# First summing stage of a graph network: half of each step's slots summed as f32 products with a widened 0/1 matrix

## The reference, cut to what matters

```python
B = jnp.exp(-edge_attr)
msgs = B[:, None] * x[col]
out = jax.ops.segment_sum(msgs, row, num_segments=N_NODES)
```

## Time and profile before

| what | value |
|---|---|
| median of 3 runs | 5168.92 us |
| lowest and highest run | 5147.55, 5176.96 us |
| span of the profiled execution, first to last instruction | 3717.5 us |
| median run less that span | 1451.4 us |
| TensorE, VectorE, ScalarE, GpSimd busy over the span | 58%, 70%, 21%, 53% |
| first and last low part of the stage (L1237) | 723.4 us, 1017.0 us |

### The profile page before, as it was taken

One profiled execution on the slowest core, in us unless ns is written; L12 is line 12 of the kernel. 1 busy time (PEld: TensorE's weight loads), 2 busy tenths in 40 slices (PEclk: granted clock), 3 DMA queues, 4 the chain that ended last, 5 costly groups with the idle time before them and its releaser, 6 DMA issues. The chain is left out here.

```text
span 3717.5 us, 94213 instructions
## 1 busy us (share of the span) xinstructions
PE 2149.9 (58%) x24555; PEld 1628.6 (44%) x24556; DVE 2606.7 (70%) x5968; ACT 796.1 (21%) x2086; POOL 1984.6 (53%) x1987
## 2 busy tenths in 40 slices
PE   1435777566535555555655553465666666666597
PEld 0225666455534444444544442344444444444232
DVE  3898999888856777776777765477777777777511
ACT  0023555455520111111111110011111111111100
POOL 0112444333327777777777730777777777776000
PEclk9867889756655666666666665566666766666699
DMA  4046777788776667666666630565555555555687
GB/s 148 12 126 170 258 260 261 233 244 237 217 74 184 184 180 190 183 175 183 186 184 182 183 94 9 130 161 146 150 151 144 153 154 148 153 148 147 223 309 282
DMA packets 679457, 646.11 MB, mean 174 GB/s; under 512 B 129015, under 2 KB 513308, under 8 KB 678333
## 3 DMA queue, kind: packets, MB, share of 16 engines
q1 hardware_dynamic: 375773, 346.64, 31.7%
q0 software_dynamic: 77184, 154.07, 17.5%
q10 hardware_dynamic: 226300, 143.41, 12.6%
HBM read 433.64 MB, written 222.40 MB: 176 GB/s over the span
## 5 line engine op out<-in xcount | busy, mean ns | idle before, releaser
L1646 POOL DMA_INDIRECT rows<-nodes_xl,id_slot x832 | 831.1, 999 | 419.3 <-issue 249.5
L1646 POOL DMA_INDIRECT rows<-nodes_kv,id_slot x832 | 825.1, 992 | 290.8 <-issue 244.8
L1842 DVE SCALAR_TENSOR_TENSOR running_counts<-running_counts,same_block,counts_p 128x128 f32<-128x128 f32 x1144 | 393.9, 344 | 412.6 <-PE counts_p L2001 305.7
L2001 PE MATMUL counts_p<-hot_src,hot_blocks 128*128 128x128 bf16 x2288 | 291.9, 281 | 585.8 <-DVE running_counts L1842 584.4
L2001 PEld LDWEIGHTS counts_p<-hot_src,hot_blocks 128*128 128x128 bf16 x2288 | 217.6, 154 | 661.4 <-DVE running_counts L1842 599.4
L2045 PE MATMUL sums<-parts,hot 128*128 128x68 bf16 (+1 forms) x4992 | 325.2, 251 | 250.1 <-DVE parts L1826 250.1
L2045 PEld LDWEIGHTS sums<-parts,hot 128*128 128x128 bf16 x4992 | 311.6, 168 | 271.5 <-issue 271.5
L1091 POOL DMA_INDIRECT msg_by_src<-message,unit_slot x156 | 199.7, 1280 | 311.3 <-DVE message L944 292.4
L1260 PE MATMUL sums<-parts,hot 128*128 128x65 bf16 x3168 | 183.7, 235 | 120.7 <-DVE parts L1237 120.7
L1687 ACT CAST parts<-mixed 128x544 bf16<-128x544 f32 (+1 forms) x208 | 133.0, 639 | 536.1 <-DVE mixed L1810 278.1
L1971 PE MATMUL picked<-rows,ident 128*128 128x512 f32 x208 | 198.2, 1054 | 79.2 <-DMA rows<-nodes_xl,id_slot 68.3
(11 more groups left out here) (490 smaller groups left out, 4289.9 us busy)
## 6 DMA issues: line engine op xcount, KB each, us to landing
hot_src<-hot_src_by_cell SPq DMA_DIRECT2D x1144, 64.0 KB
adjacency<-running_counts ACTq DMA_DIRECT2D x1144, 64.0 KB
hotT<-hotT_by_step SPq DMA_DIRECT2D x208, 256.0 KB
hot<-hot_by_step SPq DMA_DIRECT2D x208, 256.0 KB
blocks<-adjacency SPq DMA_DIRECT2D x40, 1280.0 KB
hot_src_by_cell<-hot POOLq DMA_DIRECT2D x132, 256.0 KB
loc_all<-loc_by_cell SPq DMA_DIRECT2D x104, 256.0 KB
hotT_by_step<-hotT ACTq DMA_DIRECT2D x104, 256.0 KB
```

Of the source, the lines that this page charges most:

```text
L1646: pool.indirect_dma_start(out=rows[:, j, t, :], out_offset=None, in_=table, in_offset=bass.IndirectOffsetOnAxis(ap=ids[:, j, t:t + 1], axis=0)
L1842: v.scalar_tensor_tensor(runs[:, r, q, :], before_it, same[:, bass.ds(J * BBODY + (count_from + q), 1)], counts_p[:, q - HALVES[q >= len(H ...
L2001: ins = nc.tensor.matmul(counts_p[:, q - HALVES[half][0], :], hot_b[:, r, :, t], hot_s[:, r, q, :, g], start=g == 0, stop=g == 1)
```

## The change

Of the 8 slots of a step, slots 0 to 3 (THREE = 4) go on as three bf16 parts. Slots 4 to 7 are multiplied as they arrived, in f32. For that ScalarE writes the `hot` of those four slots out in f32 (`hot_wide`, 128 x 512), in its step J for step J-1, ahead of the middle part. High part, `left`, middle part and low part have half their former size. TensorE makes 4 x 3 bf16 products and then 4 f32 products in a step. As TensorE now reads the arrived rows themselves, `load` waits for `summed` where it waited for `left_made`.

```diff
-                left = sbuf("left", [P, RS, TB, cols], ctx=c)
-                parts = sbuf("parts3", [P, RS, 3, TB, cols], BF16, ctx=c)
+                THREE = 4
+                left = sbuf("left", [P, RS, THREE, cols], ctx=c)
+                parts = sbuf("parts3", [P, RS, 3, THREE, cols], BF16, ctx=c)
+                wide = sbuf("hot_wide", [P, RS, TB - THREE, P], ctx=c)
...
                     if not known(J, RS):
-                        eng.wait_ge(left_made, J - (RS - 1))
+                        eng.wait_ge(summed, J - (RS - 1))
                         eng.wait_ge(ends_taken, J - (RS - 1))
                         eng.wait_ge(located, J - (RS - 1))
...
-                            nc.scalar.copy(parts[:, s, 0, :, :], rows[:, s, :, 0:cols]).then_inc(high_made, 1)
+                            nc.scalar.copy(parts[:, s, 0, :, :], rows[:, s, 0:THREE, 0:cols]).then_inc(high_made, 1)
                         if not known(J, 1):
+                            r = (s - 1) % RS
+                            act.wait_ge(hot_made, J)
+                            nc.scalar.copy(wide[:, r, :, :].rearrange("p (c g) e -> p c g e", g=2),
+                                           hot[:, r, THREE // 2:, :, :].rearrange("p c e g -> p c g e")).then_inc(wide_made, 1)
                             act.wait_ge(left_made, J)
                             nc.scalar.copy(parts[:, (s - 1) % RS, 1, :, :], left[:, (s - 1) % RS, :, :]).then_inc(middle_made, 1)
...
-                            v.tensor_tensor(left[:, r, :, :], rows[:, r, :, 0:cols], parts[:, r, 0, :, :], ALU.subtract).then_inc(left_made, 1)
+                            v.tensor_tensor(left[:, r, :, :], rows[:, r, 0:THREE, 0:cols], parts[:, r, 0, :, :], ALU.subtract).then_inc(left_made, 1)
...
-                        pe.wait_ge(hot_made, J + 1)
+                        pe.wait_ge(wide_made, J + 1)
                         pe.wait_ge(low_made, J + 1)
                         for b, n in enumerate(ns):
                             for t in (2 * b, 2 * b + 1):
+                                if t >= THREE:
+                                    ins = nc.tensor.matmul(sums[:, bass.ds(n, cols)], wide[:, s, t - THREE, :], rows[:, s, t, 0:cols],
+                                                           start=False, stop=False)
+                                    continue
                                 for m in range(3):
```

More of the change, by code:

```diff
@@ L1113, in aggregate @@
                 arrived = [sem(f"arrived{s}", c) for s in range(RS)]
-                located, hot_made, ends_taken, high_made, left_made, middle_made, low_made, summed = (
-                    sem(n, c) for n in ("located", "hot_made", "ends_taken", "high_made", "left_made", "middle_made", "low_made", "summed"))
+                located, hot_made, ends_taken, high_made, left_made, middle_made, low_made, wide_made, summed = (
+                    sem(n, c) for n in ("located", "hot_made", "ends_taken", "high_made", "left_made", "middle_made", "low_made",
+                                        "wide_made", "summed"))
                 own, opened, closed = sem("own", c), sem("opened", c), sem("closed", c)
```

## The result

The changed kernel takes 5438.8 us (median of 4 runs, 5429.8 to 5442.5) against 5166.3 for the kernel before: a ratio of 1.053, 95% interval 1.050 to 1.056. It is slower by 272 us, where 161 were forecast. The direction and the place were right, the size was not, and the time lies outside the range (5245 to 5400).

A forecast was written before the change was run, and what follows sets the result against it. The prediction took ScalarE's list to bound the kernel, VectorE close behind. The moved wait closes a ring, 63 x (7.04 - 4.48) = 161 us, added to 5169 for 5330 us; range 5245 to 5400.

The forecast's parts named there:

- What bounds now: Summing stage: ScalarE's list, two steps long, bounds with no slack (150.4 + 127.7 of 280 us), VectorE close behind.
- The faster rival: ScalarE's 2.20 us gap is elastic, so VectorE or transfers bound: pair 3.67 us, forecast time 5116 us; chance 0.05.
- What gets cheaper, and the widening: `left` and low part fall to 422 ns, high and middle part to 409; ScalarE's added widening takes 616 ns.
- The wait: ScalarE's loads wait for `summed` of J-1, closing a ring: pair 4.48 to 7.04 us, 63 pairs, 161 us more.
- The f32 product: TensorE's f32 products are 0.22 us apart at 1.2 GHz; a slot costs 0.22 where three bf16 products cost 0.165.
- The rule that was set aside: TensorE reloads FP32 weights in every pass: 0.43 us a product, pair about 8.8 us, time near 5430.
- the prediction's own pair: Two steps from `ends` of J at 1.2 GHz: J-1 products start 2.15, J's end 5.54, pair 7.20 us.
- The clock: TensorE's granted clock stays 0.58, about 0.16 of the time at 2.4 GHz, making the pair 7.04 us.
- The 1451 us and SyncE: The 1451 us outside the profiled span stay; SyncE's five issues per pair, now waiting for `summed`, cost nothing.

## Why the prediction was right in direction and wrong in size

**What bounds now: not refuted, and not tested.** ScalarE's list had no slack. No run shows that the stage shortens when it gets some: the two runs on the kernel before that relieve ScalarE hand its issues to SyncE, and in both SyncE's own queue, at 0.78 to 0.79 us an issue, then takes as long as the pair. With its five issues it still waited 43.1 us over the stage. The faster rival took the share of 0.82 for room down to 3.67 us a pair. Over 200 us or more of this stage no run read has more than 0.82 (40 us at its start have 0.86), and the shortest stage is still that of the kernel before. That the transfers can't go beyond this share isn't shown by it.

**What gets cheaper, and the widening: right.** 426 and 423 ns for `left` and low part (422 said), 404 for the high part (409), 614 for the widening (616).

**The wait: right.** It was called the larger term, and alone it costs 218 us. The order of starts in a pair held: first products 2.16 us after `ends` (2.15 said), 0.16 from products to issues (0.1), 1.52 to `ends` (1.56).

**The f32 product: the step that failed.** The prediction read y_new as "six in 1.55 us", "so 0.22 apart", and took 0.22 for a product. 0.22 was right for a record. But its fifty records belong to one product for each tile of 128 nodes, and 3125 nodes are 25 tiles; so a product is two records. In the changed kernel they are 1056 over the stage, for 132 x 4 products. So a product costs 0.44 us at 1.2 GHz, a slot in f32 0.44 where three bf16 products cost 0.165, and a step's issue is 0.66 + 8 x 0.22 = 2.42 us in place of 1.54. Put into the prediction's own pair: step J-1 issues from 2.15 to 4.57, J starts at 4.6, its products end 0.66 + 7 x 0.22 + 0.42 = 2.62 later, at 7.2, and with 0.1 + 1.56 the pair is 8.9. 63 x (8.9 - 4.48) = 278 us, 5447, against 5439 measured. Of the 117 us by which that exceeds the forecast 161, the price makes 63 x (8.9 - 7.2) = 107, and 10 come from taking the pair at 1.2 GHz throughout (7.20 for 7.04).

The rule that was set aside had it. The fast weight load is not used for FP32, by the Trainium skill, "TensorE: Matmul & The Clock Gate", section "Weight-path perf modes"; with the 107 ns for a load from that page's section "LDWEIGHTS" and the four passes of the Trainium skill's page "FP8 and Floating Point Precision", section "TensorE Precision Notes", the estimate was 0.43 us a product, 8.8 us a pair and a time near 5430. The trace has 0.44, 8.86 and 5439. The row did not speak against the rule; it was counted wrongly.

That it isn't the 65 columns which set the pace of a record, the trace of the kernel before shows. Eight f32 products of a later stage have weights of the same form and 128 columns in place of 64, at the same granted clock of 1.00 as the earlier trace rows:

```profile
1520.39 2.05 PE L1987 MATMUL turn_p<-ef_slot,wide_we 128*128 128x128 f32 x16
...
1520.40:1522.20 1.80, 1.80 (x17) 1.80 (x17) 0.62 (x2) 0.00 (x0) 1.38 (x2) 1.00 0.49 121
```

Sixteen records in 2.05 us, of 0.275 at the median, are (2.05 - 0.275) / 15 = 0.118 us apart; the eight records of y_new with 64 columns are (1.10 - 0.275) / 7 = 0.118 apart. Twice the columns cost nothing more. The weights are the same in both, which fits the rule; a fixed cost of a record that has nothing to do with the loads isn't excluded.

**The clock: slightly off.** 0.58 was kept, 0.50 was granted. With 0.16 of the pairs some 2 us shorter, the lower clock cost 20 us at most (an estimate), and on the side of slower than forecast.

**The 1451 us and SyncE: as costed.** The rest of the program is unchanged. SyncE's queue waited 319.5 us for products, but over the whole stage of the changed kernel ScalarE shows no wait for landings and VectorE one, of 0.8 us.

## What to carry to other kernels

When a wait is moved from one producer to a later one, follow it to the head of the issuing engine's list: if that producer depends on work which the same engine did just before, the wait closes a ring, and the buffers do not help unless the load looks ahead by fewer steps. Count records against the products in the code before a duration is taken as the price of one. An f32 product of 65 columns was no bargain against three bf16 ones: it took work from VectorE and gave it to TensorE, for which the loads now waited. And before issues are moved to another queue, see how much that queue still waits: when a run with the move has none of its waits left, the run measures that queue and not the engine that was relieved.

## What the runs showed that was not expected

- One f32 product appears as two weight loads and two matmul records, 0.22 us apart each at 1.2 GHz with 128 x 65 elements moving; three bf16 products of the same shape take 0.165 us. At 2.4 GHz f32 records are 0.118 us apart with 64 columns and with 128.
- The kernel before has executions whose spans differ by 1459 us (3717.5 and 5176.5) while this stage takes 293.6 and 295.9.
- SyncE, which has no other work, issues one of these transfers in 0.78 to 0.79 us, its register loads counted in, where its queue shows no wait for any engine. With seven of eight issues a pair on SyncE the run took 56 us more (5281.0 against 5225.3), with six 5 us more (5205.7 against 5201.1, hardly clear of the spread).
